# A quantised feed forward on one core: which engine does the last subtraction of the inner rows, and which that of the input rows

## The reference

```
def _act_quant(x):
    scale = 127.0 / jnp.clip(jnp.max(jnp.abs(x), axis=-1, keepdims=True), 1e-05)
    xq = jnp.clip(jnp.round(x * scale), -128.0, 127.0) / scale
    return x + jax.lax.stop_gradient(xq - x)

def _bitlinear(x, w):
    return jnp.einsum('bsi,oi->bso', _act_quant(x), _weight_quant(w))

gate = jax.nn.silu(_bitlinear(x, w_gate))      # 512 -> 2048
up = _bitlinear(x, w_up)                       # 512 -> 2048
return _bitlinear(gate * up, w_down)           # 2048 -> 512
```

## Time and profile before

| | |
|---|---|
| time, median of 3 runs | 1807.12 us (1805.96 to 1807.32) |
| the profiled execution: time, span | 1808.88 us, 1806.4 us |
| busy over the whole span | PE 1752.7 (97%), DVE 1412.5 (78%), ACT 1172.5 (65%), POOL 1113.4 (62%) |
| feed forward | from about 1626 us to the end |
| its loop, t = 2 to 13 | 1658.69 to 1790.38 us |

### The profile page before, as it was taken

The page is one execution under the profiler, slowest core; times in us unless marked ns, Lnnn a source line. Parts: engine busy times, 40 slices in busy tenths (PEclk is TensorE's granted clock), DMA queues, the critical chain, the costliest instruction groups (busy, mean ns, idle before and its releaser), DMA issues.

```text
span 1806.4 us, 37455 instructions
## 1 busy us (share of the span) xinstructions
PE 1752.7 (97%) x13942; PEld 1475.7 (82%) x13957; DVE 1412.5 (78%) x3240; ACT 1172.5 (65%) x2680; POOL 1113.4 (62%) x1250
## 2 busy tenths in 40 slices
PE   8999999999998899999999999999999999988997
PEld 7777777778877899999999999899899999974443
DVE  6777778787887677777777788777776777787888
ACT  6878887756755566666666667666666656654664
POOL 3434445664566586786686655677777788551554
PEclk9999999999998999999999999999999999999999
DMA  5223323111105423432432523314313341543553
GB/s 206 76 67 94 103 75 111 46 32 46 48 22 173 137 90 98 152 100 77 153 103 74 167 97 86 112 49 125 96 61 101 96 114 52 125 106 92 129 129 97
DMA packets 141106, 176.80 MB, mean 98 GB/s; under 512 B 63884, under 2 KB 99088, under 8 KB 140928
## 3 DMA queue, kind: packets, MB, share of 16 engines
q1 hardware_dynamic: 122392, 138.15, 25.3%
q0 software_dynamic: 14656, 28.92, 5.9%
q10 hardware_dynamic: 3880, 7.35, 1.3%
HBM read 109.25 MB, written 50.46 MB: 88 GB/s over the span
## 4 chain that ended last, share of the span: by engine, by line
PE 74%; DVE 10%; ACT 5%; POOL 5%; DMA 3%; issue 3%; ACTq 0%; POOLq 0%; DVEq 0%
PE att_ps_T L552 7%; PE att_ps_SA L1755 5%; PE att_ps_P L1731 5%; PE att_ps_SB L612 4%; PE att_ps_P L1719 4%; PE att_ps_P L552 4%; PE att_ps_P L1783 4%; PE att_ps_SB L600 3%; PE att_ps_O L1719 3%; PE att_ps_T L1719 3%; PE att_ps_P L1769 3%; PE att_ps_T L1731 3%; PE att_ps_O L1731 2%; PE att_ps_P L1794 2%; POOL sa_p_lo L423 2%
## 5 line engine op out<-in xcount | busy, mean ns | idle before, releaser
L1537 POOL TENSOR_TENSOR ca_pr<-ca_pr,ca_rec 112x750 f32<-112x750 f32 x256 | 366.6, 1453 | 187.2 <-DVE ca_rec L2017 184.3
L423 POOL TENSOR_TENSOR sa_p_lo<-sa_pr,sa_p_hi 112x448 fp32r<-112x448 f32 x128 | 146.8, 1162 | 210.5 <-ACT sa_p_hi L718 209.7
L1902 ACT ACTIVATE ca_big<-att_ps_P 126x384 fp32r<-126x384 f32 (+1 forms) x254 | 105.3, 449 | 66.1 <-PE att_ps_P L1769 64.9
L1896 ACT ACTIVATE ca_pr<-att_ps_SA,ca_nmax 112x750 f32<-112x750 f32 x128 | 113.7, 888 | 22.0 <-DVE ca_nmax L2013 11.2
L887 DVE RECIPROCAL sa_sums<-sa_sums 128x224 f32<-128x224 f32 x64 | 99.1, 1548 | 33.8 <-ACT sa_sums L727 33.6
L2022 DVE TENSOR_TENSOR ca_big<-att_ps_P,ca_big 126x384 fp32r<-126x384 f32 (+1 forms) x254 | 119.8, 498 | 6.2 <-ACT ca_big L1902 5.9
L2013 DVE TENSOR_REDUCE ca_nmax<-att_ps_SA 112x1 f32<-112x752 f32 x128 | 119.1, 931 | 1.3 <-PE att_ps_SA L1755 1.2
L2013 DVE TENSOR_REDUCE ca_nmax<-att_ps_SB 112x1 f32<-112x752 f32 x128 | 119.1, 930 | 0.0
L1731 PE MATMUL att_ps_P<-ca_w_hi,ca_ct 128*126 128x256 f32 x558 | 114.2, 284 | 1.4 <-DVE ca_q_lo L1996 1.4
L1896 ACT ACTIVATE ca_pr<-att_ps_SB,ca_nmax 112x750 f32<-112x750 f32 x128 | 113.3, 885 | 0.1
L1769 PEld LDWEIGHTS att_ps_P<-att_ident,ca_pr 64*126 64x126 f32 (+1 forms) x1524 | 85.5, 138 | 15.2 <-issue 10.8
(11 more groups left out here) (354 smaller groups left out, 6618.9 us busy)
## 6 DMA issues: line engine op xcount, KB each, us to landing
ct_kept<-ca_ct SPq DMA_DIRECT2D x8, 1134.0 KB, 9.3
ca_ct<-ct_kept POOLq DMA_DIRECT2D x8, 1134.0 KB, 7.7
ct_kept<-ca_ct SPq DMA_DIRECT2D x8, 1116.0 KB, 12.3
ca_ct<-ct_kept POOLq DMA_DIRECT2D x8, 1116.0 KB, 10.0
sa_xin<-in_x_dram SPq DMA_DIRECT2D x16, 448.0 KB, 3.7
xt_kept<-ca_xt SPq DMA_DIRECT2D x8, 896.0 KB, 5.2
ca_xt<-xt_kept POOLq DMA_DIRECT2D x8, 896.0 KB, 5.3
ternary<-ca_stage SPq DMA_DIRECT2D x36, 172.0 KB, 1.9
```

The lines of the kernel that those rows point to most:

```text
L423: pool.tensor_tensor(p_lo[:, h % NB, :], pr[:, h % NB, :], f32(p_hi[:, h % NB, :]), ALU.subtract).then_inc(p_split, 1)
L1537: pool.tensor_tensor(w, w, rec[:, h % PB, c:c + 1].to_broadcast([R, S]), ALU.mult).then_inc(norm_done, 1)
L1896: act.activation(pr[:, h % PB, c, :].rearrange("r (a s) -> r a s", a=2), two_halves(psum[slot]), ACT.Exp, bias=nmax[:, h % PB, c:c + 1], a ...
```

## The change

ScalarE does both halves' last subtraction of the inner rows, `quantise_hidden(t, 0)` directly behind `scale_hidden(t, 0)` and `quantise_hidden(t, 1)` behind `scale_hidden(t, 1)`, for tiles 2 to 12. VectorE does the last subtraction of the input rows for tiles 4 to 13, between `largest(t, 0)` and `hidden(t, 3)`. Tiles 0 and 1, and half 0 of tile 13, stay where they were; so do tiles 0 to 3 of the input rows.

```
-    BY_VECTOR = 3
+    BY_SCALAR = 2
@@ scalar
-        def quantise_second(t):
-            act.wait_ge(h_scaled, 2 * t + 2)
+        def quantise_hidden(t, half):
+            act.wait_ge(h_scaled, 2 * t + half + 1)
             if t:
-                act.wait_ge(hqt_in[1], 16 * t)
-            act.activation(hq[:, half_of(1)], h[:, half_of(1)], ACT.Copy, bias=-ROUND).then_inc(hq_done[1], 1)
+                act.wait_ge(hqt_in[half], 16 * t)
+            act.activation(hq[:, half_of(half)], h[:, half_of(half)], ACT.Copy, bias=-ROUND).then_inc(hq_done[half], 1)
...
             for t in range(1, T):
                 scale_hidden(t - 1, 0)
+                if t > BY_SCALAR:
+                    quantise_hidden(t - 1, 0)
                 scale_hidden(t - 1, 1)
-                quantise_second(t - 1)
+                quantise_hidden(t - 1, 1)
                 silu(t, 0)
                 silu(t, 1)
                 if t + 2 < T:
                     round_x(t + 2)
                 silu(t, 2)
-                if t + 2 < T:
+                if t == 1:
                     quantise_x(t + 2)
                 silu(t, 3)
@@ vector
         def quantise_x(t):
             dve.wait_ge(xr_done, t + 1)
-            if t:
-                dve.wait_ge(xt_filled, t)
+            if t <= BY_TENSOR:
+                if t:
+                    dve.wait_ge(xt_filled, t)
+            else:
+                dve.wait_ge(*before_x(t))
             dve.tensor_scalar(xq[:, :], xr[:, :], -ROUND, None, ALU.add).then_inc(xq_done, 1)
...
                 largest(t, 0)
+                if t + 2 < T:
+                    quantise_x(t + 2)
                 hidden(t, 3)
                 scale_of_hidden(t)
                 guess_root(t - 2, sums)
-                quantise_hidden(t, 0)
+            quantise_hidden(T - 1, 0)
             quantise_hidden(T - 1, 1)
```

## The result

The changed kernel takes 1815.81 us (median of 6 runs, 1814.63 to 1817.59), the kernel before beside it 1808.28 us (6 runs, 1805.96 to 1810.02). The ratio is 1.0041, interval 1.0031 to 1.0052: slower by 5.6 to 9.4 us. The profiled execution took 1815.94 us with a span of 1814.2, against 1808.88 and 1806.4.

A forecast was written before the change was run, and what follows sets the result against it. Bound: a loop alternating between VectorE and ScalarE, 10.90 us per iteration, PE near. Terms 0.47 + 0.35 = 0.82 per full iteration; 0.35 + 0.63 + 6.56 + 0.77 + 1.06 = 9.4 us slower, 1816.5 us, range 1811.5 to 1822.

The forecast's parts named there:

- ScalarE's idle time lies behind the silus, the addition ahead of them: ScalarE's 3.9 us idle per iteration would not hide the added subtraction; first silu moves from 3.18 to 4.27.
- VectorE's relief does not shorten the loop: VectorE gives up 1.66 us per iteration for 0.35, yet the full iteration grows by 0.82 us.
- The silus: ScalarE's first silu comes 1.09 us later; 0.62 goes into the vanished `xscale` wait, 0.47 per iteration stays.
- `xq` on VectorE 0.35, nothing covers it: Input rows' last subtraction between VectorE's third `hidden` and `hscale`, where it has no gap: 0.35 us per iteration.
- t = 12, 13: 0.77 and 1.06: Last two iterations, without `round_x` and `xq`: third `hidden` at 6.63 instead of 5.86 and 5.57.
- t = 2: 0.35: Iteration 2 gets only the added `xq` on VectorE: 0.35 us longer.
- DMAs: 0: Transposes of `hq` and `xq` shift in issue time but arrive before they are needed: no cost.
- t = 3: 0.63: Iteration 3, whose third `hidden` already came late for PE at 6.68: 0.63 us longer.
- VectorE was the bound and is relieved: Rival: ScalarE's idle time hides the addition, PE then bounds the loop at 10.35, total 1801.7 us; chance 0.04.
- `xq` did not meet GpSimd: Rival: `xq` on VectorE collides with GpSimd's second large operation or store, 0.51 us ten times, 1821.6 us; chance 0.07.
- PE's clock: Rival: TensorE idling some 1.4 us per iteration lowers its clock, total 1819 to 1820.5 us; chance 0.04.

The follow-up runs named there:

- e4: Changed kernel with ScalarE's `round_x` moved behind the third silu: middle iteration 11.39 us, ratio 1.0040 to the kernel before.
- e3: Kernel before with `round_x` moved behind the third silu and ScalarE's `xq` behind the fourth: middle iteration 10.90 us, ratio 1.0003.
- e2: Changed kernel with half 0's last subtraction of the inner rows back on VectorE, `xq` staying there: middle iteration 11.24 us, ratio 1.0014 to the kernel before.
- e6: Changed kernel with VectorE's `xq` moved to the start of its next iteration, where it waits for GpSimd: middle iteration 11.20 us, ratio 1.0027 to the kernel before.
- e8: Changed kernel with `xq` at VectorE's iteration start, both inner scalings before both subtractions, `round_x` behind third silu: middle iteration 10.77 us, ratio 1.0002 to the kernel before.
- e1: Changed kernel with the input rows' last subtraction (`xq`) back on ScalarE: middle iteration 11.20 us, ratio 1.0020 to the kernel before.
- e7: Changed kernel with both ScalarE scalings of the inner rows ahead of both last subtractions: middle iteration 11.24 us, ratio 1.0022 to the kernel before.
- e5: Kernel before with VectorE's `scale_of_x` for the next tile moved ahead of half 0's last subtraction: middle iteration 10.36 us, ratio 0.9984.

## Why the prediction was right

The forecast was +9.4 us, 1816.5 and a range of 1811.5 to 1822; measured are 1815.81 and a ratio of 1.0041, 7.4 us. That it came so near is in part luck: in the profiled executions the middle iterations were forecast 1.8 us too long, and t = 3 came out 0.8 us longer than forecast, most of it by the clock, as told below. Point by point:

- *ScalarE's idle time lies behind the silus, the addition ahead of them.* Right, and it decided the sign. The first silu was put at 4.27 and is at 4.27.
- *VectorE's relief does not shorten the loop.* Right in the changed kernel, where VectorE waits 1.28 us for GpSimd and 0.48 for the first silu.
- *The silus: third silu 0.77 behind `round_x`, third `hidden` at 6.96, so 0.47.* The way through ScalarE's queue was right for the changed kernel (e4), but the term was mis-sized, because the path read from the kernel before was wrong at one link: it had `round_x` hold the third silu there. The term is 0.30 to 0.31, with the third silu 0.61 behind `round_x` and the third `hidden` at 6.80. The 0.77 of the earlier trace rows held a wait of 0.16 for VectorE's first `hidden`, in which the profile names no releaser, and e3 showed it: without `round_x` in front the third silu starts at the same offset, 5.72. Over eight iterations this is 1.3 us of the 1.8 by which the middle was forecast too long.
- *`xq` on VectorE 0.35, nothing covers it.* 0.33, and e2 and e6 show that the place is the price.
- Of the rest of the middle's miss, 0.3 us is the iteration t = 9 of the kernel before, which lasted 11.20 and was counted as 10.90.
- *t = 12, 13: 0.77 and 1.06.* 0.80 and 1.08.
- *t = 2: 0.35.* It was 0.17 in these two traces; the ten have 12.70 to 13.07 there.
- *DMAs: 0.* Right, though the transpose of half 1 of `hq` was issued at 4.39 and not, as forecast, about 1 us later than before: there it was issued at 4.32, behind the load of the residual.
- *t = 3: 0.63.* It was 1.43. TensorE's clock, and not the change, made up the most of that: all ten traces have TensorE idle for 4.82 to 4.98 us in iteration 2, and granted 1.2 GHz for a while behind it. The window over the 16 matmuls of `down` that follow, in the kernel before and in the changed one:

```profile
1668.50:1672.70 4.20, 4.20 (x17) 1.78 (x16) 3.47 (x12) 1.16 (x2) 0.45 (x1) 0.82 0.14 31
```

```profile
1667.50:1673.00 5.50, 5.50 (x17) 2.10 (x16) 3.69 (x13) 2.21 (x3) 1.27 (x3) 0.62 0.11 24
```

  The mean granted clock is 0.82 and 0.62, and the 16 matmuls took 4.17 and 5.50 us (1668.58 to 1672.75, 1667.55 to 1673.05). Of the ten traces the changed kernel's, e3's and e8's show the longer form, with 12.51, 12.23 and 12.17 us for t = 3; the other seven have 10.94 to 11.39. In e1, e4, e6 and e7, which have the shorter form, t = 3 lasts as long as a middle iteration, within 0.02 us. An estimate for the changed kernel without the longer form is thus 11.53, which is 0.45 above before where 0.63 was forecast; the rest, 0.98, is the clock. It goes with neither the order nor the division of the work; what decides it stays open.
- *Rivals.* "VectorE was the bound and is relieved" fell with e1: given the relief and not `xq`, the loop still lasts 11.20 us. Its first half was true: e5 shows that VectorE's chain was the bound; what came back from it was taken by ScalarE's addition. `xq` did not meet GpSimd (all its 13 instances take 0.41 to 0.43 us). PE's clock stayed at 1.00 in the loop, though PE waited 1.0 us in each iteration where it had waited 0.36. Forecast were 1.3 to 1.4, with an iteration 0.2 us longer than it came out.

## What to carry to other kernels

Where two engines alternate in a loop, neither the busy shares nor the sum of an engine's idle time says what a moved operation costs. Write down one iteration as offsets, and look whether the operation goes into the stretch between a result and the next one that waits for it, or into the gap. The same operations on the same engines gave 11.53 us in one order and 10.77 in another; and moving a step that waits for nothing into a wait (e5) gained what dividing the work anew had not. When a distance between two instructions is carried over from a trace to a new order, look first whether it contains a wait: 0.77 us was 0.61 us and a wait of 0.16.

## What the runs showed of the hardware

- A VectorE operation of only 128x2 elements is held by a GpSimd operation too: in e5 `ff_x_unit` took 0.84 us beside GpSimd's 1.03 us operation, from 1732.64 to 1733.48, which ended at 1733.45; the median of its 14 instances in the kernel before is 0.22. The 128x1 operations in front of it and behind it took 0.16 and 0.14, as always. The Trainium skill, SBUF — State Buffer, section Who interferes with whom, says that a `tensor_scalar` in a two-port mode and a GpSimd operation exclude each other, whichever is issued first holding the other up for its whole length. The trace agrees, in that GpSimd's started first and VectorE's ended 0.03 us behind it; that VectorE's ran in such a mode no run shows.
- The subtraction of half 0 on VectorE was not of one length: 0.69 alone and 1.20 beside GpSimd. Where GpSimd's operation had waited for its store to land, and so started only 0.04 to 0.09 us ahead of the subtraction, it was 1.49 (t = 9 in the kernel before) and 1.54 (e3). In all three it ended 0.55 to 0.56 us behind GpSimd's. In t = 12 of the kernel before the subtraction started first, at 1771.33, and took 0.69; GpSimd's operation, from 1771.55, took 1.37 instead of 1.03. The longer subtraction is the odd iteration of 11.20 or 11.25 us in the kernel before and in e3, which the changed kernel doesn't have.
- After about the same idle time, 4.8 to 5.0 us, TensorE ran at the lower clock for two different times: the 16 matmuls behind it took 4.0 to 4.3 us in seven traces and 5.3 to 5.5 in three, which moved one iteration by 1.0 to 1.4 us.
